# The last pair of attention heads transposed by TensorE, and the work around it put in another order

## What is computed

```python
sa, ca, ga, sb, cb, gb = (silu(c) @ wmod).split(6)      # ga and gb keep their sign and are at least 0.25 in size
h = layernorm(x) * (1 + ca) + sa
attn = softmax(causal(rope(h @ Wq.T) @ rope(h @ Wk.T).T / 8)) @ (h @ Wv.T)
x = x + ga * (attn @ Wo.T)                              # Wo: 256 x 2048
h = layernorm(x) * (1 + cb) + sb
w = scatter(softmax(top2(h @ gate_w.T)))                # two of 8 experts for each row
base1, base3 = h @ w1.T, h @ w3.T                       # 704 wide
for A1, B1, A3, B3, A2, B2, we in experts:              # rank 16
    act = silu(base1 + 2 * h @ A1.T @ B1.T) * (base3 + 2 * h @ A3.T @ B3.T)
    out += we * (act @ w2.T + 2 * act @ A2.T @ B2.T)
x = x + gb * out
```

## Time and profile before

| | |
|---|---|
| median of 3 runs | 452.83 us (452.75 to 453.12) |
| profiled execution | 453.68 us, of which the span between first and last instruction is 451.9 us |
| TensorE busy | 427.8 us, 95% of the span |
| VectorE, ScalarE, GpSimd busy | 360.6, 349.4 and 343.4 us |
| mean granted clock of TensorE | 0.992 of full speed |

### The profile page before, as it was taken

One profiled execution on the slowest core, in us unless ns is written; L12 is line 12 of the kernel. 1 busy time (PEld: TensorE's weight loads), 2 busy tenths in 40 slices (PEclk: granted clock), 3 DMA queues, 4 the chain that ended last, 5 costly groups with the idle time before them and its releaser, 6 DMA issues.

```text
span 451.9 us, 12333 instructions
## 1 busy us (share of the span) xinstructions
PE 427.8 (95%) x4509; PEld 308.4 (68%) x4509; DVE 360.6 (80%) x994; ACT 349.4 (77%) x643; POOL 343.4 (76%) x306
## 2 busy tenths in 40 slices
PE   7989999899999999999999998998979989999994
PEld 4557676687877888778788786886946444554562
DVE  5978798598898889888889998998866778545666
ACT  5688999699899899989989979989854456743441
POOL 5677999996699986769999897864416794486692
PEclk9999999899999999999999999999999989999999
DMA  8465426647142685334358332265120000000001
GB/s 291 147 212 192 141 49 189 160 134 198 26 118 59 189 222 143 94 72 138 87 135 205 105 86 72 71 189 96 25 48 0 1 1 2 0 1 0 25 23 49
DMA packets 58108, 45.13 MB, mean 100 GB/s; under 512 B 36856, under 2 KB 49600, under 8 KB 58048
## 3 DMA queue, kind: packets, MB, share of 16 engines
q1 hardware_dynamic: 57440, 43.67, 35.8%
q10 hardware_dynamic: 608, 0.66, 0.4%
HBM read 23.93 MB, written 11.54 MB: 78 GB/s over the span
## 4 chain that ended last, share of the span: by engine, by line
PE 64%; POOL 14%; DVE 6%; ACT 5%; issue 4%; DMA 4%; SPq 2%; ACTq 0%; DVEq 0%; POOLq 0%
PE ps L575 10%; PE ps L490 9%; PE ps L492 9%; PE ps L491 9%; PE ps L556 5%; PE ps L558 5%; PE ps L821 3%; PE ps L599 3%; PE ps L603 3%; PE ps L601 3%; DMA oT<-on_l 2%; POOL raw L1675 2%; POOL rot L1675 2%; PE ps L851 2%; POOL rot L1694 2%
## 5 line engine op out<-in xcount | busy, mean ns | idle before, releaser
L1024 ACT ACTIVATE prob<-prob,least 128x512 f32<-128x512 f32 (+3 forms) x256 | 122.4, 553 | 0.0
L1376 DVE CUSTOM_DVE_ANT_0 prob<-ps,causal 128x512 f32<-128x512 f32 (+3 forms) x256 | 117.4, 484 | 5.9 <-PE ps L558 4.6
L1384 DVE SCALAR_TENSOR_TENSOR pl<-ps,ph 128x512 f16<-128x512 f32 (+1 forms) x128 | 105.0, 820 | 21.4 <-ACT ph L1031 18.1
L1031 ACT ACTIVATE ph<-ps 128x512 f16<-128x512 f32 (+1 forms) x128 | 86.9, 700 | 22.8 <-PE ps L575 20.4
L575 PE MATMUL ps<-ident,prob 128*128 128x128 f32 x640 | 81.9, 274 | 0.6 <-DVE pl L1384 0.6
L556 PE MATMUL ps<-kT_h,qT 128*128 128x512 f16 (+3 forms) x256 | 76.4, 301 | 3.8 <-DVE least L1376 3.4
L575 PEld LDWEIGHTS ps<-ident,prob 128*128 128x128 f32 x640 | 69.0, 142 | 1.9 <-DVE pl L1384 1.3
L558 PE MATMUL ps<-kT_l,qT 128*128 128x512 f16 (+3 forms) x256 | 70.0, 300 | 0.0
L599 PE MATMUL ps<-vh,ph 128*128 128x65 f16 x640 | 64.9, 194 | 0.4 <-DVE pl L1384 0.4
L601 PE MATMUL ps<-vl,ph 128*128 128x64 f16 x640 | 64.9, 193 | 0.0
L603 PE MATMUL ps<-vh,pl 128*128 128x65 f16 x640 | 64.8, 193 | 0.0
(11 more groups left out here) (220 smaller groups left out, 999.5 us busy)
## 6 DMA issues: line engine op xcount, KB each, us to landing
spill<-rot SPq DMA_DIRECT2D x20, 512.0 KB, 3.2
wst<-chunks SPq DMA_DIRECT2D x30, 256.0 KB, 4.3
qT<-spill SPq DMA_DIRECT2D x15, 512.0 KB, 3.7
kT_h<-spill SPq DMA_DIRECT2D x6, 256.0 KB, 3.8
xs<-x SPq DMA_DIRECT2D x2, 512.0 KB, 5.7
oT<-wmod SPq DMA_DIRECT2D x2, 512.0 KB, 8.7
raw<-chunks SPq DMA_DIRECT2D x4, 256.0 KB, 4.5
out<-xs SPq DMA_DIRECT2D x4, 256.0 KB, 2.2
```

The source lines that it names most:

```text
L1024: act.activation(prob[:, m % 2, c], prob[:, m % 2, c], ACT.Exp, bias=least[:, m % 2, qt:qt + 1], scale=-1.0).then_inc(exp_done, 1)
L1376: ins = dve.tensor_tensor_reduce(prob[:, m % 2, at:at + w], ps[:, bank, off:off + w], causal[:, S - w:S], -1.0 / HD ** 0.5, 3.0e38, ALU.ad ...
L1384: dve.scalar_tensor_tensor(out=pl[:, m % 2, c], in0=ps[:, PT_BANK:PT_BANK + 3, :].rearrange("p a b -> p (a b)")[:, c], scalar=PROB_SCALE, ...
```

## The change

Four things are edited. The pair's transposes: for pair 31 alone, `output_high`, `output_low` and SyncE's two transfers go. TensorE transposes the fp32 `on` into PSUM bank 1 (four transposes of 128x128), ScalarE copies the bank to `oT`'s high part, and VectorE subtracts to get the low part. The semaphore `g_mm` is named `turned` and counts both this and an earlier use. TensorE's order: the four transposes stand between the two LoRA inputs, the last outputs between these, the masks and `h_base(0, 0)`. VectorE's order: the sum of batch 6 comes first, the low part of `oT` stands between the first and the second choice, and the sums of outputs 0 and 1 come before the mask inputs. ScalarE's order: the copy stands ahead of the masks, and the table load moves behind `tm_high(0, (0, 1))`.

```diff
-            transpose_outputs(PAIRS - 1)
...
-            lora_inputs(0, (0, 1))
-            mask_transposes(0, (0, 1))
+            lora_inputs(0, (0,))
+            pe.wait_ge(normed, HEADS)
+            for t in range(T):
+                mm = pe.transpose(ps[:, 1, t * P:(t + 1) * P], on[:, (PAIRS - 1) % 2, t, :], ident[:, :])
+            mm.then_inc(turned, 1)
+            lora_inputs(0, (1,))
+            last_output(0)
+            mask_transposes(0, (0,))
+            last_output(1)
+            mask_transposes(0, (1,))
             h_base(0, 0)
             mask_transposes(0, (2,))
-            last_output(0)
-            last_output(1)
+            last_output(2)
+            last_output(3)
             h_lora(0, 0)
             mask_transposes(0, (3, 4))
-            last_output(2)
-            last_output(3)
             h_base(0, 1)
...
-                if n >= 1 and n % 2 == 1:
+                if n >= 1 and n % 2 == 1 and n < HEADS - 1:
                     output_high(n // 2)
...
+            act.wait_ge(turned, 2)
+            act.wait_ge(op_done, 4 * (PAIRS // 4 - 2))
+            act.activation(oT[:, 0, (PAIRS - 1) % 8, :], ps[:, 1, :], ACT.Copy).then_inc(oT_landed[(PAIRS - 1) % 8], 16)
             act.wait_ge(s_done, 3 * HEADS)
             choice_wide(0, 0)
             choice_wide(0, 1)
             weights_exp(0)
             choice_wide(0, 2)
-            act.activation(c_e[:, :, :], c_sb[:, :, :], ACT.Silu)
             masks_out(0, (0, 1))
             weights_wide(0)
             tm_high(0, (0, 1))
+            act.activation(c_e[:, :, :], c_sb[:, :, :], ACT.Silu)
             masks_out(0, (2,))
             tm_high(0, (2, 3))
...
+            op_add(W - 1, 3, MISC_BANK)
             first_choice(0)
+            dve.wait_ge(oT_landed[(PAIRS - 1) % 8], 32 * ((PAIRS - 1) // 8) + 16)
+            dve.tensor_tensor(oT[:, 1, (PAIRS - 1) % 8, :], ps[:, 1, :], oT[:, 0, (PAIRS - 1) % 8, :], ALU.subtract)\
+               .then_inc(oT_landed[(PAIRS - 1) % 8], 16)
             second_choice(0)
             choices_difference(0)
-            op_add(W - 1, 3, MISC_BANK)
             weights(0)
+            op_add(W, 0, MISC_BANK + 1)
+            op_add(W, 1, MISC_BANK)
             dve.wait_ge(fs["mT"], 2)
             mask_input(0, 0)
             mask_input(0, 1)
...
-            op_add(W, 0, MISC_BANK + 1)
-            op_add(W, 1, MISC_BANK)
...
-                if n >= 2 and n % 2 == 0:
+                if n >= 2 and n % 2 == 0 and n < HEADS:
                     output_low(n // 2 - 1)
```

More of the change, by code:

```diff
@@ L278, in block_kernel @@
         hl_first, hl_second, ht_dve = sem("hl_first"), sem("hl_second"), sem("ht_dve")
-        g_s, g_a, g_m, g_mm, g_out, g_written, g_ready = (sem(f"g_{k}") for k in ("s", "a", "m", "mm", "out", "written", "ready"))
+        g_s, g_a, g_m, turned, g_out, g_written, g_ready = (sem(f"g_{k}") for k in ("s", "a", "m", "turned", "out", "written", "ready"))
         wh_ready, wl_ready = sem("wh_ready"), sem("wl_ready")
@@ L693, in _ @@
                     pe.transpose(ps[0:2 * B * DK, PV_BANK, 0:P], g_abs[:, :, :, :].rearrange("p i b k -> p (i b k)"), ident[:, :])\
-                      .then_inc(g_mm, 1)
+                      .then_inc(turned, 1)
                 if n == 56:
@@ L1449, in _ @@
                 if n == GATES_AT:
-                    dve.wait_ge(g_mm, 1)
+                    dve.wait_ge(turned, 1)
                     dve.tensor_copy(g_rows[:, :], ps[0:2 * B * DK, PV_BANK, 0:P]).then_inc(g_out, 1)
```

## The result

| | before | after |
|---|---|---|
| median, measured together, 18 runs each | 453.84 us (452.18 to 455.77) | 450.65 us (448.77 to 454.28) |
| ratio | | 0.9932, 95% interval 0.9914 to 0.9951 |
| profiled execution, its span | 453.68 us, 451.9 us | 449.73 us, 447.9 us |
| mean granted clock of that execution | 0.992 | 0.994 |
| first LoRA product to `h_base(0, 1)` | 15.83 us | 14.32 us |

The kernel is 3.1 us faster (0.68%; interval 2.2 to 3.9 us). The forecast of 451.0 us lies 0.35 us from the median, but partly by luck: it started from a median of 452.83 us, which in this and the later, larger measurements of the kernel before is 453.5 to 454.1 us, and it allowed a gain of 1.8 us.

What follows compares the result with a forecast made beforehand. TensorE was taken as the bound, almost without a gap from 338.24 to 367.4. Waits of 2.55 us less 0.44 and 0.3 gave 1.8 us: 453.68 to 451.88, less 0.85 to the median, 451.0 us; range 450.2 to 452.2.

Steps and rivals of the forecast that it cites:

- The waits that go, 2.55 us, less 0.44 us of transposes: TensorE ahead of masks 0, 1 and output 0: waits of 0.97, 1.06 and 0.52 us go; four added transposes cost 0.44.
- the 2.03 us for the choice: TensorE's waits for `wide`, the choice of experts, ahead of masks 0 and 1: 2.03 of the 2.55 us.
- A new wait of 0.3 us: TensorE ahead of output 0, waiting for VectorE's low part of `oT`: 0.3 us; rival of up to 1.1 us, chance 0.11.
- the first choice's 0.19 us in place of 1.15: VectorE's L1474, ahead of the subtraction: took 1.15 us beside GpSimd's `on_l`, expected at 0.2 us without it.
- 0.1 us for handing over: Allowance on the new route through ScalarE and VectorE, added after the subtraction's end at 333.06: about 0.1 us.
- The table load costs nothing, with 1.5 us of cover: ScalarE's moved load delays mask 2; mask inputs end at 342.3, `h_base(0, 1)` asks at 343.85: cover 1.5 us, nothing lost.
- All of it reaches the end: TensorE runs almost without a gap from 338.24 to 367.4, so the 1.8 us won before 345.65 reach the end.
- GpSimd's cover is thin: Second batch row's route: GpSimd done at 350.3, its next low part due at 350.6, cover 0.3 us.
- the short idle time that was to be left ahead of `av_l`: On GpSimd, ahead of the second `av_l`: an idle time, if short, was expected to remain.
- The total: Whole kernel: 453.68 us profiled becomes 451.88, less 0.85 us to the median: 451.0 us, chance 0.70.
- The three runs lie within 0.37 us: Argument against both clock rivals: the spread of the kernel's runs speaks against a fall that comes only in some.
- no clock fall: Rival: TensorE's clock fall behind the stop ahead of `gate_logits(1)` doesn't come, saving 1.5 us more: 449.5 us, chance 0.07.

Runs made afterwards that it cites:

- order_only: Changed kernel's new orders on all engines, but the last pair goes through the DMA transposes as before; 456.89 us, ratio 1.0070 to the kernel before.
- pair_only: Changed kernel's transposes of the last pair on TensorE, with outputs, masks, sums and table load in their old order; 453.49 us, ratio 0.9989 to the kernel before.
- load_back: Changed kernel with the table load at its old place, ahead of mask copies 0 and 1; 449.69 us, ratio 0.9912 to the kernel before.
- dve_one: Kernel before with one small copy more on VectorE ahead of its first choice; 453.05 us in one run.
- shifted: Changed kernel with seven more unread products of 512 columns ahead of the last pair's transposes; 452.99 us, ratio 0.9982 to the kernel before.
- after_again: The changed kernel itself, measured once more beside others; 451.12 us, ratio 0.9944 to the kernel before.

## Why the prediction was right, and where it was off

**The waits that go, 2.55 us, less 0.44 us of transposes.** Right, each of them. There is no idle time ahead of masks 0, 1 and 2, and the transposes took 0.44 us. `order_only` shows what the prediction's sum left open, that the order needs the quick route: the outputs can fill the 2.03 us for the choice only if the pair is there in time. That the route in turn needs the order is shown only for the place of the subtraction that `pair_only` has.

**A new wait of 0.3 us.** Mis-sized: it is 0.62 us. Copy (0.60) and subtraction (0.69) were right, also the first choice's 0.19 us in place of 1.15. I had taken 0.1 us for handing over; the rows show 0.13 us between ScalarE and VectorE, 0.25 us between VectorE and TensorE, and 0.04 us more ahead of the copy. So 2.55 - 0.44 - 0.62 = 1.49 us, against 1.51 measured.

**The table load costs nothing, with 1.5 us of cover.** Right: 1.4 us of cover. `load_back` adds that its old place would have cost nothing either. Between the load's start and mask 2's copy lie 1.41 us with `c_e` between them, as before; a drain of 1.38 us on top, as the Trainium skill has it ("ScalarE: Activation LUTs", What ACT_TABLE_LOAD costs), doesn't show in either place.

**All of it reaches the end; GpSimd's cover is thin.** Right, though the short idle time that was to be left ahead of `av_l` isn't listed: the stop ahead of `gate_logits(1)` is 1.87 us, and from `h_base(0, 1)` to it are 23.63 us in both.

**The total.** The step that failed is the one from the profiled execution to the median, with the clock: "The three runs lie within 0.37 us, which they would not if the fall came in some and not in others". The falls do come in some and not in others; 18 runs of the kernel before span 3.6 us, and the three had just been alike. So the price of the clock is no fixed part of the kernel but a mean over its executions, and the base was 1 us low. The rule of the Trainium skill that I set aside ("TensorE: Matmul & The Clock Gate", Part 1), that the windows run freely and don't start with the kernel, agrees with this trace: the same code behind the same 2.2 us stop ran at 0.50 in one execution and at 1.00 in the other. The rival "no clock fall" was one of these cases taken as the whole kernel, and its price of 1.5 us was too high: the same stretch with and without the fall differs by 0.9 to 1.2 us (the one at 86 cost 1.7).

**What the sum lacked.** 0.72 us at the tail, since one more instruction on VectorE takes a fetch of instructions out of the last store. This part of the gain is luck: it has nothing to do with the idea of the change, and `dve_one` gets the same from a copy that does nothing. With 1.51 us it makes 2.23 us, which is also what lies between the two kernels' runs at equal clock (2.23 us, standard error 0.18). The median gain, 3.1 us, is 0.9 us more. The mean clock is 0.9954 over 30 runs of the changed kernel against 0.9933 over 74 of the kernel before, 0.0020 apart at standard errors of 0.0007 and 0.0004. A straight line through each kernel's runs gives 1.2 to 1.5 us per 0.004 of clock, hence 0.6 to 0.75 us. That falls have become rarer is measured; why they have is not settled. Part of it may lie ahead of the diff: the fall near 86 to 88 is in all six profiles whose stretch was 15.7 us or longer and in four of the eight with 14.0 to 14.3 us, a split that chance alone gives in 7 of 100 cases. `shifted` points to the place in time at which the later stops come, not to the stops removed, yet by a window that ran wholly free the place should not matter. This stays open.

## What to carry to other kernels

A stall is read at the engine that waits, by starts: of a chain of nearly 8 us through norm, copies and transfer only 0.52 us were TensorE's, and the rest of its idle time belonged to another chain. Reordering can be worth something only together with a shorter route (here it cost 3 us alone), so price them together and try them apart; and when an order is tried without its partner, move what was placed for the partner too. Count a hand-over between engines at 0.13 to 0.25 us each, and where the clock falls in some executions, compare twenty runs of each kernel and read their clocks before the base of a sum is taken from three.

## What the runs showed of the hardware that I had not expected

- Instructions are fetched while the kernel runs (a packet of 8 KB is the last one seen here), and when the last fetch comes can hang on a single instruction. One small copy more on VectorE moved it from 3.4 us behind the start of TensorE's last product to 0.5 us, out of the last store's data, and shortened the tail by 0.72 us (5.33 to 4.61 us), from one profile each, with the same two values in fourteen profiles: 5.33 to 5.35 in three, 4.60 to 4.62 in eleven. In the three the fetch came in the middle of the last store, whose last packet then ended 0.6 us later. That these packets stood behind the fetch on its DMA engine is inferred from their order; so is that a block of instructions ends at another place.
- TensorE's clock fell behind stops of 1.9 to 2.1 us at 366 to 374 in some profiles and not in others (`after_again` had a stop of 1.87 us there and no fall, `shifted` one of 1.91 us and a fall); of thirteen profiles that kept this stop seven show the fall. At one of 4.13 us it fell while TensorE still stood and stayed at its lower level for nearly seven microseconds (336.2 to 343.1).
- Behind the stops ahead of the masks (0.81 and 0.89 us in the earlier trace rows, 1.56 us in `pair_only`) no profile shows a fall.
